# Where the shared down product's bias is added, and x1 in two buffers

## What is computed

```python
x = x + _L0_xattn_ref(_layernorm(x), ctx_512, Wq, Wkv_expand, Wout)
x = x + _L0_ffn_ref(_layernorm(x), ...)

def _L0_ffn_ref(hidden_states, router_w, wg, wu, wd, sg_w, sg_b, su_w, su_b, sd_w, sd_b):
    logits = x @ router_w.T
    scores, top_idx = jax.lax.top_k(logits, K)
    ...
    moe_out = jnp.einsum('etd,te->td', y, comb)
    se = jax.nn.silu(x @ sg_w + sg_b) * (x @ su_w + su_b) @ sd_w + sd_b
    out = (moe_out + se)
```

## Time and profile before

| | |
|---|---|
| median of 3 runs | 796.08 us (795.2 to 797.45) |
| profiled execution | 795.9 us, span 793.8 us, mean granted clock 0.995 |
| PE busy | 761.3 us (96% of the span) |
| DVE, ACT, POOL busy | 73%, 58%, 55% |
| starts of the additions to x1 (line 667) | 52.4 to 354.7 us |
| starts of the base loads (line 458) | 341.9 to 467.6 us |
| starts of the gathers (line 716) | 447.0 to 763.4 us |

### The profile page before, as it was taken

The page is one execution under the profiler, slowest core; times in us unless marked ns, Lnnn a source line. Parts: engine busy times, 40 slices in busy tenths (PEclk is TensorE's granted clock), DMA queues, the critical chain, the costliest instruction groups (busy, mean ns, idle before and its releaser), DMA issues.

```text
span 793.8 us, 21959 instructions
## 1 busy us (share of the span) xinstructions
PE 761.3 (96%) x7249; PEld 521.5 (66%) x7249; DVE 580.4 (73%) x1194; ACT 460.9 (58%) x847; POOL 435.7 (55%) x563
## 2 busy tenths in 40 slices
PE   4998999999999999999999999999999999999995
PEld 2767878878888888778888874455554555555552
DVE  5899989999999998855898775565555555565552
ACT  4786889989898889775556332333333333333330
POOL 3454687777777777563210203656555555656543
PEclk9999999999999999999999999999999999999998
DMA  8326668787776777868846746979898999889892
GB/s 292 127 78 178 198 185 221 212 234 206 203 210 209 210 197 204 232 178 255 263 159 213 231 156 123 155 137 152 144 151 157 139 153 149 154 134 164 145 147 35
DMA packets 138318, 140.73 MB, mean 177 GB/s; under 512 B 87872, under 2 KB 88896, under 8 KB 137856
## 3 DMA queue, kind: packets, MB, share of 16 engines
q1 hardware_dynamic: 122336, 104.01, 49.3%
q0 software_dynamic: 15904, 35.70, 26.2%
HBM read 71.61 MB, written 52.31 MB: 156 GB/s over the span
## 4 chain that ended last, share of the span: by engine, by line
PE 78%; DMA 3%; ACT 1%; issue 1%; SPq 1%; DVE 1%; POOL 0%; POOLq 0%; ACTq 0%
PE psum L1431 44%; PE psum L1495 18%; PE psum L1422 9%; PE psum L1545 4%; PE psum L1588 2%; DMA hidT<-xn2p 2%; DMA out<-w_q,tabs 1%; DMA probsT<-normed_turned 0%; PE psum L1567 0%; SPq L515 0%; PE psum L1570 0%; SPq L520 0%; DVE w_q L1411 0%; PE psum L1609 0%; PE psum L1548 0%
## 5 line engine op out<-in xcount | busy, mean ns | idle before, releaser
L726 POOL DMA_INDIRECT out<-w_q,tabs x71 | 112.5, 1585 | 109.9 <-DVE w_q L1411 76.9
L716 POOL DMA_INDIRECT x_in<-normed_tokens,tabs x71 | 71.2, 1003 | 89.6 <-DVE tabs L1292 42.2
L917 ACT ACTIVATE silu_g<-psum,tabs 128x256 f32<-128x256 f32 x71 | 33.7, 474 | 146.5 <-PE psum L1431 138.3
L1396 DVE SCALAR_TENSOR_TENSOR hid<-psum,tabs,silu_g 128x256 f32<-128x256 f32 x71 | 34.4, 484 | 111.8 <-ACT silu_g L917 110.3
L1431 PE MATMUL psum<-exp_all,hidT 128*128 x426 | 103.4, 379 | 2.6 <-DMA hidT<-xn2p 2.6
L1431 PE MATMUL psum<-exp_all,probsT 128*128 x420 | 96.4, 379 | 0.0
L1495 PE MATMUL psum<-xn1T,w_q 128*128 128x128 f16 x1536 | 91.0, 219 | 0.8 <-DVE maxima L949 0.8
L1431 PE MATMUL psum<-w_o,attnT 128*128 128x512 f16 x384 | 88.0, 379 | 0.8 <-DVE w_o L966 0.4
L1495 PEld LDWEIGHTS psum<-xn1T,w_q 128*128 128x128 f16 x1536 | 86.3, 98 | 2.1 <-issue 2.0
L572 POOL TENSOR_TENSOR exp_all<-piece,exp_all 128x512 f32 (+1 forms) x48 | 56.0, 1166 | 45.1 <-ACT piece L746 45.1
L1431 PEld LDWEIGHTS psum<-exp_all,hidT 128*128 128x128 f16 x426 | 41.6, 98 | 53.2 <-issue 4.3
(11 more groups left out here) (216 smaller groups left out, 1648.7 us busy)
## 6 DMA issues: line engine op xcount, KB each, us to landing
x_in<-x SPq DMA_DIRECT2D x64, 256.0 KB, 3.2
exp_all<-experts SPq DMA_DIRECT2D x24, 512.0 KB, 5.2
out<-xy SPq DMA_DIRECT2D x32, 256.0 KB, 3.2
normed_tokens<-xn SPq DMA_DIRECT2D x32, 256.0 KB, 5.1
normed_turned<-xn2T SPq DMA_DIRECT2D x32, 256.0 KB, 3.7
w_q<-out SPq DMA_DIRECT2D x32, 256.0 KB, 3.1
out<-w_q SPq DMA_DIRECT2D x32, 256.0 KB, 2.6
probsT<-normed_turned SPq DMA_DIRECT2D x16, 256.0 KB, 3.6
```

Source lines behind the costliest of these rows:

```text
L716: pool.indirect_dma_start(x_in[:, t % 4, :], None, xn_dram, bass.IndirectOffsetOnAxis(gather_at[:, t:t + 1], 0)).then_inc(gathered[t % 4], 16)
L726: pool.indirect_dma_start(out, bass.IndirectOffsetOnAxis(add_at[:, t:t + 1], 0), y[:, t % Y_RING, :], None, bounds_check=TOKENS - 1, oob_i ...
L917: act.activation(silu_g[:, :], psum[:, GU_BANK[m % 2], 0:I], ACT.Silu, scale=gate_scale_at[:, tm:tm + 1]).then_inc(silu_ready, 1)
L1396: dve.scalar_tensor_tensor(hid[:, :], psum[:, GU_BANK[m % 2], I:2 * I], up_scale_at[:, tm:tm + 1], silu_g[:, :], ALU.mult, ALU.mult).then_ ...
```

## The change

Line 667 goes. x1 has two buffers, the two halves of `xy`, used by turns; SP stores x1 itself into the output as soon as it is there, and `base_stored` becomes two semaphores. DVE's x1 waits for the store and the normalization of the tile two before. The bias is added to the base when it has come back: `add_bias(n)` on POOL, in place in `y`, and DVE's line 1404 waits for that instead of the load.

```diff
-        x1, base = xy[:, 0, :], xy[:, 1, :]
...
 # SP, step
-                    sp.wait_ge(x1b_ready, t5 + 1)
-                    sp.dma_start(out[bass.ds(t5 * P, P), :], base).then_inc(base_stored, 16)
+                    sp.wait_ge(x1_ready, t5 + 1)
+                    sp.dma_start(out[bass.ds(t5 * P, P), :], xy[:, (j + 1) % 2, :]).then_inc(base_stored[(j + 1) % 2], 16)
...
 # SP, load_base
-                sp.wait_ge(base_stored, 16 * (n + 1))
+                sp.wait_ge(base_stored[n % 2], 16 * (n // 2 + 1))
...
 # POOL
+            def add_bias(n):
+                if n == 0:
+                    pool.wait_ge(bias_in, 32)
+                pool.wait_ge(base_back[n % Y_RING], 16 * (n // Y_RING + 1))
+                pool.tensor_tensor(y[:, n % Y_RING, :], y[:, n % Y_RING, :], sd_bias[:, :], ALU.add).then_inc(y_biased, 1)
...
 # POOL, step
                 if live(t4):
                     inv_std(1, t4)
-
-                    pool.wait_ge(x1_ready, t4 + 1)
-                    wait(pool, base_stored, 16 * t4)
-                    if isinstance(t4, int) and t4 == 0:
-                        pool.wait_ge(bias_in, 32)
-                    pool.tensor_tensor(base, x1, sd_bias[:, :], ALU.add).then_inc(x1b_ready, 1)
...
             for tile in range(T, T + LAG):
                 step(tile // TPB, tile % TPB)
-
+                if tile > T + 2:
+                    for n in range(2):
+                        add_bias(2 * (tile - T - 3) + n)
...
-            for k in range(PIECES):
-                low_piece(E - 1, k)
-
+            for n in range(6, T - 4):
+                if 0 <= n - ROUTE_AT - 1 < PIECES:
+                    low_piece(E - 1, n - ROUTE_AT - 1)
+                add_bias(n)
             pool.wait_ge(gather_ready, 1)
...
-            for t in range(SLOTS + ADD_BEHIND):
+            for t in range(4):
+                gather(t)
+                add_bias(T - 4 + t)
+            for t in range(4, SLOTS + ADD_BEHIND):
...
 # ACT, step
-                    act.activation(xn2[:, (j + 1) % 2, 0:H], x1, ACT.Identity, bias=rstd[:, 1, 2:3],
+                    act.activation(xn2[:, (j + 1) % 2, 0:H], xy[:, (j + 1) % 2, :], ACT.Identity, bias=rstd[:, 1, 2:3],
...
 # DVE, step
-                    wait(dve, x1b_ready, t4)
-                    wait(dve, xn2_ready, t4)
+                    wait(dve, base_stored[j % 2], 16 * (TPB // 2 * b + j // 2 - 2))
+                    wait(dve, xn2_ready, t4 - 1)
+                    plain(dve)
+                    x1 = xy[:, j % 2, :]
...
 # DVE, entry
-                        dve.wait_ge(base_back[k % Y_RING], 16 * (k // Y_RING + 1))
+                        dve.wait_ge(y_biased, k + 1)
```

More of the change, by code:

```diff
@@ L268, in xattn_moe @@
             "probsT_mm", "probsT_hi", "probsT_ready", "av_mm", "recip_ready", "attn_ready")]
-        attnT_mm, attnT_hi, attnT_ready, proj_mm, x1_ready, x1b_ready = [sem(n) for n in (
-            "attnT_mm", "attnT_hi", "attnT_ready", "proj_mm", "x1_ready", "x1b_ready")]
-        xn2_ready, xn2_hi, xn2_parts, xn2_turned, xT_stored, router_mm, logits_ready, logits_stored, base_stored = [
+        attnT_mm, attnT_hi, attnT_ready, proj_mm, x1_ready = [sem(n) for n in (
+            "attnT_mm", "attnT_hi", "attnT_ready", "proj_mm", "x1_ready")]
+        xn2_ready, xn2_hi, xn2_parts, xn2_turned, xT_stored, router_mm, logits_ready, logits_stored = [
             sem(n) for n in ("xn2_ready", "xn2_hi", "xn2_parts", "xn2_turned", "xT_stored", "router_mm",
-                             "logits_ready", "logits_stored", "base_stored")]
+                             "logits_ready", "logits_stored")]
+        base_stored, y_biased = [sem(f"base_stored{i}") for i in range(2)], sem("y_biased")
         xn2_stored = [sem(f"xn2_stored{i}") for i in range(2)]
```

## The result

| | before | after |
|---|---|---|
| median (6 runs each) | 795.71 us (795.2 to 797.72) | 811.25 us (807.77 to 814.71) |
| ratio of the times | | 1.0189, 95% interval 1.0165 to 1.0212 |
| profiled execution, span | 795.9, 793.8 us | 810.55, 808.8 us |

What follows compares the result with a forecast made beforehand. The prediction took PE, busy for 96% of the span, to bound the kernel. Its terms -3.0 + 16.4 + 0.8 = +14.2 on the profiled 795.9 us gave 810 us, range 801 to 816.

Steps and rivals of the forecast that it cites:

- Steps: Step loop and just before: line 667's additions leaving POOL end waits of PE, -3.0 us (0 to -3.6).
- First place: Steps T+3 and T+4: additions behind low pieces delay y(0) and y(2), putting PE 4.3 us behind.
- Second place, the ring: Entries 10 to 16: low pieces behind additions awaiting loads delay silu; 10.8 us per two entries, silu(15) 16.4 late.
- What reaches PE: After entries 10 to 16: silu(15)'s whole lateness reaches PE, 16.4 us (ends 13.5 and 16.4).
- a stretch of 0.8: Entries 10 to 16: DVE's route work slowed beside POOL's work, 0.8 us on the path (ends 0 and 2.4).
- The sign that missed: PE's gaps between 355 and 430 us were to add up to 16 to 17 us.
- Rival 3, the clock: PE's clock drops in the new gaps, two drops costing some +3: 812 to 818 us, chance 0.16.
- Rivals 1 and 2: Only the delay at steps T+3 and T+4 counts, 797.2 us, chance 0.10; faster, only -3.0 left, 792.9 us, chance 0.06.

Runs made afterwards that it cites:

- e6: The kernel before without line 667: SP stores x1 itself from its one buffer, the bias is left out; 794.36 us, ratio 0.9998.
- e2: The changed kernel with each low piece of the last expert two places earlier, additions kept; 798.46 us, ratio 1.0048.
- e5: The changed kernel with every addition on y cut to one column, at its place and with its waits; 803.58 us, ratio 1.0121.
- e7: The kernel before with one wait more: POOL waits for the load of base 10+k ahead of each low_piece(7,k); 803.67 us, ratio 1.0126.
- e3: The changed kernel with the last expert's low pieces two places earlier and the first additions earlier too; 795.15 us, ratio 1.0014.
- e1: The changed kernel without any of the 32 additions on y, y waiting for the load itself; 792.38 us, ratio 0.9972.
- e10: e3 with every addition cut to one column; 790.71 us, ratio 0.9946.
- e9: e3 with the last low piece moved behind the addition for tile 14, and that addition waiting for y(13); 796.86 us, ratio 1.0009.

## Why the prediction was right, point by point

- **Steps, -3.0.** Measured -3.01 at the first product behind them, and the two gaps that the term was added up from are gone. The size held. I put it all on POOL's emptied place and x1's second buffer at nothing; by e6 that is too simple, and how much needs the second buffer stays open.
- **First place, 4.3.** Measured 3.57, by the mechanism named: y(0) waited for POOL behind low_piece(6,3), then y(2) behind low_piece(6,5).
- **Second place, the ring.** Forecast, less the 3.0: silu(11) at 391.6, silu(13) 11.3 later, silu(15) 13.7 later. Measured 393.52, 10.4 and 13.9. The first was late because the load for tile 10, issued at 384.67, let the addition start only at 389.79, 5.1 us, where I had taken 3.1. The rounds behind it were shorter than forecast (the last one without its stretch, below), in part because their loads took 2.7. e2 (place), e5 (length) and e7 (the wait alone) show that it is the load ahead of the low piece that makes the ring, and that the addition's 1.275 us is the smaller part.
- **What reaches PE, 16.4 and a stretch of 0.8.** Measured 18.0. Two stretched rows lie on its path: the scan at 405.73, 1.62 in place of 0.69, and the row at 419.22, 1.07 in place of 0.42, together 1.6 us. That is within the ends of 0 and 2.4; both ran beside low pieces (405.65 and 418.86 on POOL), not beside additions. The other 16.4 meets the forecast by luck: the first load took 2.0 us more than forecast, and the rounds and the end took as much less. What the prediction calls gate and up of entry 17 is that of tile 17, which stands in entry 18; the entries 15 and 17 of the earlier trace rows are likewise tiles 15 and 17.
- **The sign that missed.** PE's listed gaps between 355 and 430 us add up to 13.7, not 16 to 17, for the two slow rows filled 3.07 us in which PE would have waited.
- **Rival 3, the clock.** Its condition came in part, its price of "some 3" did not. The clock stayed full behind the first place and fell twice in the second; behind the last round too, where the rival let it count, PE still had to wait for y(13). The Trainium skill (TensorE: Matmul & The Clock Gate, Part 1) has such a fall after idle time; the trace agrees for the gaps of 3.45 and 2.83. Gaps of 2.02 and 2.39 us were followed by the full clock, unlike the one of 1.99 in the kernel before and one of 2.18 in e3, so the length of the gap alone does not decide; what else counts, no run here shows.
- **Rivals 1 and 2.** The first, that only the first place counts, comes nearest to e2, the changed kernel with the low pieces out of the ring: 3.8 us over the kernel before, where the rival has 1.3. The second, faster, is e1 and e10, with the additions gone or cut short.

The spans of the two profiled executions differ by 15.0 us where the sum has 14.2; the 0.8 over is the second stretched row. The median of 811.25 lies 1.25 from the forecast, and the six times behind it run from 807.77 to 814.71.

## What to carry to other kernels

Before moving work on an engine with idle time, ask what is queued behind its new wait: here a piece of weights that nobody needed for hundreds of microseconds stood behind a load, and through a single buffer it held up ACT, DVE and at last PE, in a ring with a longer period than the pipeline's. Put work with no hurry but with a consumer behind a buffer ahead of waits, not behind them. And an engine that looks half idle may share a resource with a full one: 1.27 us on POOL took about 1 us from DVE at the moment they met.

## What the runs showed of the hardware

- A DVE row that meets a POOL addition of 1.27 us may end only after it: 1.44 in place of 0.42 us, 1.28 in place of 0.20 for a cast with one input (e3), 1.52 in place of 0.74 (e9). Beside additions of 0.19 us the first two lasted 0.41 and 0.19 (e10).
- A gap of 3.45 us in PE was followed by a granted clock of 0.66 and 0.50 (1.2 GHz) in the next stretches, one of 2.83 by 0.63 and 0.51; gaps of 2.02 and 2.39 us by none, and one of 2.18 in e3 by 0.59 and 0.56.
- A slow stretch of PE costs nothing where PE's next wait is for work that does not hang on it: 4.28 us of products and a wait of 0.76 in the changed kernel, 2.85 and 1.99 in e7.
